# Moving five scatters and two weight splits in the instruction order of a one-core attention and mixture-of-experts kernel

## The reference, cut to what matters

```python
xn = layernorm(x)
# attention: 16 heads of 32, chunks of 128 tokens
q, k, v = silu(xn @ Wq), silu(xn @ Wk), silu(xn @ Wv)
scores = (q_chunk @ k_chunk.T) * D                # decay, causal
o = scores @ v_chunk + (q_chunk @ S) * q_decay
S = chunk_decay * S + (k_chunk * k_decay).T @ v_chunk
o = o * sigmoid((xn @ Wg1) @ Wg2)
o = o * rsqrt(mean(o * o per head) + EPS) * norm_w
attn = o @ Wo
# experts: top 2 of 8, 1280 slots each, two matmuls 512 -> 2048 -> 512
e, gate = top_k(softmax(xn @ Wg), 2)
slot = running count of the tokens that chose e   # dropped past 1280
moe = sum over the 2 choices of gate * (relu(xn @ w1[e]) @ w2[e])
out = x + attn + moe
```

## Time and profile before

| | |
|---|---|
| median of 3 runs | 2051.6 us (2050.61 to 2053.07) |
| the profiled execution | 2050.61 us |
| its span, first to last instruction | 2048.7 us |
| TensorE busy | 2013.3 us, 98% of the span |
| VectorE, GpSimd, ScalarE busy | 906.7, 731.3, 552.7 us |
| TensorE on the chain that ended last | 96% |
| mean granted TensorE clock | 0.995 of full speed |

### The profile page before, as it was taken

One profiled execution on the slowest core, in us unless ns is written; L12 is line 12 of the kernel. 1 busy time (PEld: TensorE's weight loads), 2 busy tenths in 40 slices (PEclk: granted clock), 3 DMA queues, 4 the chain that ended last, 5 costly groups with the idle time before them and its releaser, 6 DMA issues.

```text
span 2048.7 us, 27795 instructions
## 1 busy us (share of the span) xinstructions
PE 2013.3 (98%) x11096; PEld 1659.5 (81%) x11096; DVE 906.7 (44%) x1791; ACT 552.7 (27%) x985; POOL 731.3 (36%) x600
## 2 busy tenths in 40 slices
PE   7999999999999999999999999999999999999996
PEld 6788888888888888888888888888888888888885
DVE  7776777776752224324323422422342234324311
ACT  5322222223332123123212312421242123123210
POOL 4454535553632214233242431332142224324211
PEclk9999999999999999999999999999999999999998
DMA  7012021202352125224233421531162125224021
GB/s 233 31 63 84 24 82 63 84 17 89 94 161 48 34 47 159 36 64 109 70 68 65 133 45 53 127 67 30 47 158 39 40 49 154 40 60 116 21 30 20
DMA packets 85500, 151.36 MB, mean 74 GB/s; under 512 B 18304, under 2 KB 18304, under 8 KB 85360
## 3 DMA queue, kind: packets, MB, share of 16 engines
q1 hardware_dynamic: 61312, 105.64, 16.0%
q0 software_dynamic: 24048, 43.76, 12.6%
HBM read 109.82 MB, written 39.53 MB: 73 GB/s over the span
## 4 chain that ended last, share of the span: by engine, by line
PE 96%; DVE 2%; issue 1%; POOL 1%; ACT 0%; DMA 0%; SPq 0%; ACTq 0%; POOLq 0%
PE bank L1199 50%; PE bank L1463 34%; PE bank L1322 4%; PE bank L1498 2%; PE bank L1248 2%; PE bank L1206 1%; PE bank L1289 1%; PE bank L1311 1%; PE bank L1305 1%; DVE oT_lo L981 0%; DVE xnT_lo L864 0%; PE bank L1282 0%; ACT oT_hi L716 0%; POOL out_rows L612 0%; PE bank L1333 0%
## 5 line engine op out<-in xcount | busy, mean ns | idle before, releaser
L1146 DVE SCALAR_TENSOR_TENSOR h_lo<-bank,h_hi 128x512 fp32r<-128x512 f32 x256 | 176.7, 690 | 758.8 <-ACT h_hi L804 716.3
L599 POOL DMA_INDIRECT gathered<-xn_rows,gather_row x304 | 321.7, 1058 | 475.0 <-DVE x_blocks L1022 294.1
L1199 PE MATMUL bank<-xT_hi,w_hi 128*128 128x512 f32 x1024 | 398.7, 389 | 0.3 <-issue 0.2
L1199 PE MATMUL bank<-xT_hi,w_lo 128*128 128x512 f32 x1024 | 398.4, 389 | 0.0
L1199 PE MATMUL bank<-xT_lo,w_hi 128*128 128x512 f32 x1024 | 398.4, 389 | 0.0
L1463 PE MATMUL bank<-w_hi,h_hi 128*128 128x512 f32 x1024 | 398.3, 389 | 0.0
L1463 PE MATMUL bank<-w_lo,h_hi 128*128 128x512 f32 x1024 | 398.3, 389 | 0.0
L1463 PE MATMUL bank<-w_hi,h_lo 128*128 128x512 f32 x1024 | 398.3, 389 | 0.0
L804 ACT ACTIVATE h_hi<-bank 128x512 fp32r<-128x512 f32 x256 | 153.0, 597 | 813.3 <-PE bank L1199 729.6
L612 POOL DMA_INDIRECT out_rows<-y,add_row x80 | 128.6, 1608 | 550.4 <-ACT y L797 477.5
L1199 PEld LDWEIGHTS bank<-xT_hi,w_hi 128*128 128x128 f32 x1024 | 192.2, 188 | 41.4 <-issue 1.7
(11 more groups left out here) (195 smaller groups left out, 2354.1 us busy)
## 6 DMA issues: line engine op xcount, KB each, us to landing
raw_weights<-in_L_ffn_w SPq DMA_DIRECT2D x256, 256.0 KB
x_in<-in_L_attn_x SPq DMA_DIRECT2D x32, 256.0 KB
xn_rows<-xn SPq DMA_DIRECT2D x32, 256.0 KB, 2.7
x_res<-in_L_attn_x SPq DMA_DIRECT2D x32, 256.0 KB
out_rows<-y_attn SPq DMA_DIRECT2D x28, 256.0 KB, 2.0
gathered<-xn_rows,gather_row POOLq DMA_INDIRECT x304
out_rows<-y,add_row POOLq DMA_INDIRECT x80, 5.9
attn_raw<-in_L_attn_Wq SPq DMA_DIRECT2D x4, 256.0 KB, 5.0
```

The source lines that it names most:

```text
L599: pool.indirect_dma_start(xg[:, nth % 2, q * P:(q + 1) * P], None, xn_pieces, bass.IndirectOffsetOnAxis(ap=gather_row[:, col, q:q + 1], ax ...
L1146: v_.scalar_tensor_tensor(h_lo[f % 2][:, 0:n * P], h_bank[f % 2][:, 0:n * P], 0.0, h_hi[f % 2][:, 0:n * P].bitcast(F32), ALU.max, ALU.subt ...
L1199: last = mm(dest, at(left[l], t), at_r(right[r], t), start=(i == 0), stop=(i == n - 1))
```

## The change

Three things are moved; none is added or taken away, but for one wait.

1. GpSimd, super-tiles 1 to 7: the first five scatters of a super-tile are issued at the end of the unit before its first one, as soon as the slots are known, and no longer wait for `scored` of the first unit. In that first unit `head_scales(u-1)` comes ahead of `decayed_k(u+1)` and not between it and `decayed_q(u+1)`. The last three scatters stay behind `decayed_q(u+1)`.
2. GpSimd, super-tile 0: four scatters are issued ahead of `norm_scale(2)` and `norm_scale(3)`, where three were issued behind them. Four, where there were five, stay behind `decayed_q(1)`.
3. VectorE: `split_low(0, 4)` and `split_low(0, 5)` move from between `first_low(2)` and `first_low(3)` to unit 30, between `oT_low(28)` and `gate_output(30)`.

```diff
@@ gpsimd
+            for t, r in ROUTES[:4]:
+                route(0, t, r)
             norm_scale(2)
             norm_scale(3)
             for u in range(ATTN_UNITS):
                 g, i = u // GROUPS, u % GROUPS
-                ahead = 5 if g else 3
-                if i == 0:
-                    pool.wait_ge(S["scored"], u + 1)
-                    for t, r in ROUTES[:ahead]:
-                        route(g, t, r)
-                if u > 0 and i > 0:
+                if u > 0:
                     head_scales(u - 1)
                 if u < ATTN_UNITS - 1:
                     decayed_k(u + 1)
-                    if u > 0 and i == 0:
-                        head_scales(u - 1)
                     decayed_q(u + 1)
                 if i == 0:
-                    for t, r in ROUTES[ahead:]:
+                    for t, r in ROUTES[5 if g else 4:]:
                         route(g, t, r)
...
                 if i == GROUPS - 1 and g < SUPERS - 1:
                     if g < SUPERS - 2:
                         norm_scale(2 * (g + 2))
+                    for t, r in ROUTES[:5]:
+                        route(g + 1, t, r)
@@ vector
+                if u == ATTN_UNITS - 2:
+                    split_low(0, FPC)
+                    split_low(0, FPC + 1)
                 gate_output(u)
...
-            for i in range(BLOCKS[0] - 1):
+            for i in range(BLOCKS[0]):
                 first_low(i)
-            split_low(0, FPC)
-            split_low(0, FPC + 1)
-            first_low(BLOCKS[0] - 1)
```

## The result

| | before | changed |
|---|---|---|
| median (4 runs each, same chip) | 2051.39 us (2050.61 to 2053.07) | 2081.05 us (2079.36 to 2081.8) |
| profiled execution, its span | 2050.61, 2048.7 us | 2078.62, 2076.8 us |
| mean granted TensorE clock | 0.995 | 0.995 |

The ratio is 1.0137, interval 1.0125 to 1.0148: slower by 1.4%, where I forecast 0.18% and ended my range at 2057.4. The spans differ by 28.1 us.

What follows compares the result with a forecast made beforehand. TensorE, busy 2013.3 of 2048.7 us, was taken as the bound, so only its waits count. 2.4 - 1.1 + 0 + 2.3 = +3.6 us gave 2055.2 us, 0.18% slower; range 2052.8 to 2057.4.

Steps and rivals of the forecast that it cites:

- The seven borders, "Cost and gain: 0": Borders between super-tiles: earlier scatters and moved head scales neither delay TensorE nor help it, 0 us.
- rival 3: Borders: kdT 0.4 us late at six or seven of them, +2.8, sum +6.4, 2058.0 us; chance 0.08.
- rival 4: Super-tile 0: scatters queue behind the fill of the output's spare rows, normalise 1.8 us later, +5.4, 2057.0 us; chance 0.08.
- Super-tile 0, "2.4 us": Unit 0: early scatters wait for the table's fill and delay normalise, the states and TensorE's attend(0) by 2.4 us.
- my upper value of 0.75: Super-tile 0: upper bound in us of the step from fill landing to first scatter, giving a 3.0 us delay.
- The gain of 1.06: Super-tile 0, unit 2: one scatter fewer ahead of the head scales removes TensorE's wait for kdT, 1.06 us.
- The splits, "2.3 us": Units 30 and 31: two splits ahead of gate_output(30), slowed by GpSimd's kdT, delay TensorE by 2.3 us.
- The three terms of the sum that are not 0: Super-tile 0's delay +2.4, its gain at unit 2 -1.1, and the splits' delay +2.3 us.

Runs made afterwards that it cites:

- e17: The changed kernel, unaltered, in a single execution beside another kernel's repeated ones: 2058.28 us.
- B: The occasion of the first four follow-up runs, which tried parts of the change, four to ten runs each: 2053.66 to 2072.98 us.
- e1: Kernel before with only the border part of the change (early scatters, new place of the head scales): 2072.98 us, 1.0107.
- e2: Kernel before with only the new place of the head scales at the borders, scatters waiting for the scores again: 2062.57 us, 1.0056.
- E: The occasion of four kernels with five early scatters at the borders, four timed runs each on one chip: 2069.98 to 2077.35 us.
- e15: Kernel before with five early scatters at the borders and the old place of the head scales: 2072.01 us, 1.0109.
- e16: Kernel before with the border part of the change, plus GpSimd's wait for the scores behind the five early scatters: 2070.09 us, 1.01.
- e3: Kernel before with only the super-tile 0 part, four scatters ahead of the first two norm scales: 2055.68 us, 1.0022.
- e9: The changed kernel, unaltered, run once more in a single execution: 2058.05 us.
- e13: The changed kernel, unaltered, timed again beside three others on one chip: 2077.35 us, 1.0132.
- e4: Kernel before with only the two splits moved to unit 30: 2053.66 us, 1.0012.
- A: The occasion of the result, the changed kernel beside the one before: 2081.05 against 2051.39 us.
- e8: Kernel before with eight unused GpSimd memsets where the early border scatters would stand, scatters behind the scores: 2078.98 us.
- e12: Border part of the change with the new place of the head scales but no early border scatter, all eight behind decayed_q: 2055.66 us.

## Why the prediction was wrong

**The seven borders, "Cost and gain: 0".** This is the step that failed, by 20.7 us. Its arithmetic was right: in e17 the early scatters run from 98.04 to 104.21, and the rows of GpSimd and VectorE there are

```profile
98.04 1.07 POOL L545 DMA_INDIRECT slot_table<-record,slot_no  x1 [3.12 <-DVE slot_no L937]
...
104.23 2.94 POOL L553 TENSOR_TENSOR head_scale<-mean_sq,minus_half 128x16 f32<-128x16 f32 x1
107.60 1.28 POOL L501 TENSOR_TENSOR kdT<-kT,k_decay 128x512 f32<-128x512 f32 x1 [0.42 <-ACT kT L685]
...
100.03 2.49 DVE L887 TENSOR_TENSOR scores<-bank,intra_decay 128x512 f32<-128x512 f32 x4 [1.84 <-PE bank L1245]
```

with the step of 0.8 us, kdT waiting for its input and not for the head scales, and no wait of TensorE. What it assumed without a row was that a scatter beside the scores costs the scores nothing. Before's trace has scatters beside other signals of TensorE, and they cost those nothing, but none that was under way when the scores' signal was due. On the occasion of the result that signal came up to 3.9 us late, and those behind it up to 4.7. No rival had it: rival 3 put the delay into kdT (+2.8 in all), rival 4 into the fill. Both looked for it in a queue of GpSimd, and it was in the handing over of signals between other engines. That the early scatters are what it takes, and not the head scales, is shown for B (e1 against e2) and E (e15, e16, with old order and with a wait). Why the delay is there on three occasions and absent on three is open, and so is its mechanism: what holds the signal back is not shown.

**Super-tile 0, "2.4 us".** Right in kind, too small: the new wait was 3.0 us (e3, e17) or 4.1 (changed, e9), and 2.3 in e13. The step behind the fill was 0.9 us, beyond my upper value of 0.75; I took 0.2, which was the step behind GpSimd's own arithmetic. In changed and e9, kdT fell on the last `normalise` besides, 1.0 us, in e17 and e3 on the first instruction of the states, 0.4 to 0.9. The forecast had kdT at unit 1 out of the sum. Then the clock: its fall after the idle time added 1.7 us, and no term had it. Behind its start, before never stood still for that long, so no row could have priced it. Its trace could have: after TensorE's waits in the fill of the pipeline (9.3 and 2.6 us) the clock stood at 0.50 from 16.20 for 3.4 us.

**The gain of 1.06** was 1.14 to 1.17 in every run that had it. **The splits, "2.3 us"**: +2.3 in the changed kernel and in e4, 2.36 us for the two beside the row that it was read from. In e9, e13 and e17 the clock fell behind that wait as well, in e17 to 0.50 from 556 to 558 us, and the place cost 3.8 to 4.0. In the changed kernel and in e4 it did not fall there. Nothing in the experts took the shift up.

**The port of VectorE and GpSimd.** By the Trainium skill, page "SBUF — State Buffer", section "SBUF: two separate sides", GpSimd can't write the descriptors of its own DMAs while VectorE runs an operation that uses both ports. If `normalise` is such an operation, which no row shows, this would have held back the early scatters while it ran. The traces do not bear it out, as far as a scatter's record shows. In before a scatter ran from 41.60 to 42.66, wholly beside the four `normalise` of the earlier trace rows (41.55 to 43.45), and took 1.06 us, where most take 0.97. At the border of the changed kernel the two overlap by 0.15 us only, and the scatter took 1.07 (1.04 in the earlier trace rows).

**Without the late signals** the change is at 2058.05 and 2058.28 us, +8.4 on 2049.69 and 2049.89. The forecast was +3.6; the missing 4.8 are the longer wait (0.6 to 1.7), and two falls of the clock (about 1.7 each). So even there my range, which ended 5.8 above the median of before, was too narrow. The three terms of the sum that are not 0 had the right signs, by the mechanisms that I had named for them.

## What to carry to other kernels

An idle time of an engine off the path is not free room: a DMA moved into it runs beside signals that other engines exchange there. That other signals had stood beside such a DMA without harm said nothing for the one that mattered here, so time that move alone. A wait that you add to TensorE can have a second price behind it, here from 1.7 us of waiting on, so set its upper bound with a fall of the clock, 1.7 us, added. And measure a kernel on more than one occasion before you explain 1%: one and the same text stood at +8 and at +28 us.

## What the runs showed of the hardware

- On three occasions (A, B, E), where an early scatter was under way when the scores' signal was due at a border, that signal was raised 2.3 to 3.9 us after its matmul, and the following ones, until the five scatters were through, 1.7 to 4.7 us. At super-tile 0 it was 0.41 (e3) and 2.33 us (e13). Signals beside scatters that had begun behind the scores' were at most 0.18 us late in the same traces. On the three other occasions all were 0.13 us late at most.
- A scatter that had waited for the table's fill began 0.9 us after its landing, one that had waited for VectorE 0.8 us after its end; one that followed another began 0.30 us after its end.
- After an idle TensorE of 4.1 us (changed, e9) the granted clock stood at 0.50 for some 3.4 us. After 3.0 us it fell in e17 and did not in e3's profile. After 2.3 to 2.6 us it fell at all seven borders of e8, and once each in e1, e12 and e13; after 2.4 us at two borders of the changed kernel it did not. After waits of 1.6 to 1.7 us it fell at one border of e2 and not at the other six, nor at those of the changed kernel. So the length of one wait does not decide it in these traces.
- A scatter and VectorE's `normalise` ran side by side in before: 1.06 us for the scatter, 1.90 for the four `normalise`. GpSimd's kdT beside them made them 1.0 us longer (2.91), and beside the first instruction of the states that one 0.4 to 0.9 us.
